# Decoder layer, second quantisation: block 0 rounded, turned and copied alone, block 1 behind the first MLP chunk

## What is computed

```python
x = _layernorm(x + attn(x, Wi, Wf, Wg, w_norm, Wo))          # "1" in the kernel's names
x = _layernorm(x + wkv(w, u, k=x, v=ctx))                    # "2"
x = _layernorm(x + ffn(x, w_gate_up, w_down))                # "3"

def ffn(x, w_gate_up, w_down):
    xq = quant(x)                       # per token: round(x / s) * s, s = max|x| / 127
    gate, up = split(xq @ quant(w_gate_up).T)                # 1408 each
    h = silu(gate) * up
    return quant(h) @ quant(w_down).T
```

## Time and profile before

| | before |
|---|---|
| time, median of 3 runs | 444.82 us (441.57 to 445.95) |
| the profiled execution: its time / its span | 447.09 us / 445.3 us |
| PE busy | 368.4 us (83%) |
| DVE busy | 367.7 us (83%) |
| ACT busy | 321.1 us (72%) |
| POOL busy | 233.1 us (52%) |
| chain that ended last, by engine | ACT 23%, PE 21%, DVE 20%, issue 18%, POOL 10%, DMA 5% |
| mean granted TensorE clock | 0.931 of 2.4 GHz |

### The profile page before, as it was taken

The page is one execution under the profiler, slowest core; times in us unless marked ns, Lnnn a source line. Parts: engine busy times, 40 slices in busy tenths (PEclk is TensorE's granted clock), DMA queues, the critical chain, the costliest instruction groups (busy, mean ns, idle before and its releaser), DMA issues.

```text
span 445.3 us, 7315 instructions
## 1 busy us (share of the span) xinstructions
PE 368.4 (83%) x2462; PEld 284.6 (64%) x2484; DVE 367.7 (83%) x620; ACT 321.1 (72%) x421; POOL 233.1 (52%) x283
## 2 busy tenths in 40 slices
PE   4895689299939989989998999899989998558773
PEld 4894579189736577748775877577757885224331
DVE  2869529966798889998989898979898989899684
ACT  4487286656954789859884988498859985886762
POOL 3436442463364475468446843673477437635550
PEclk8697888779997999999999999989999999978998
DMA  8659635136301002030203020302011101000101
GB/s 299 269 188 180 104 116 177 47 131 66 118 23 74 0 1 72 1 119 1 72 1 118 3 71 1 116 2 70 0 67 50 59 12 59 11 26 0 49 4 68
DMA packets 13340, 31.70 MB, mean 71 GB/s; under 512 B 4864, under 2 KB 4864, under 8 KB 13312
## 3 DMA queue, kind: packets, MB, share of 16 engines
q1 hardware_dynamic: 13312, 31.35, 23.3%
HBM read 27.14 MB, written 4.21 MB: 70 GB/s over the span
## 4 chain that ended last, share of the span: by engine, by line
ACT 23%; PE 21%; DVE 20%; issue 18%; POOL 10%; DMA 5%; POOLq 0%; ACTq 0%; DVEq 0%; SPq 0%
PE proj_ps L460 14%; PE slot_ps L561 4%; DMA ring<-w_gate_up_dram 3%; POOL ring L1207 3%; ACT L921 2%; ACT hqT L894 2%; ACT turn_ps L834 2%; ACT L925 2%; DVE inp L1396 2%; ACT ring L880 2%; DVE x_max L1512 2%; POOL x_low L1130 2%; ACT gate L775 2%; ACT turn_ps L842 1%; POOL gate L1147 1%
## 5 line engine op out<-in xcount | busy, mean ns | idle before, releaser
L561 PE MATMUL slot_ps<-w1q,xqT 128*128 128x512 bf16 (+1 forms) x377 | 84.4, 376 | 10.2 <-ACT xqT L871 7.6
L460 PE MATMUL proj_ps<-x_high,proj_high 128*128 128x256 f32 x384 | 67.3, 299 | 7.7 <-DVE inp L1415 3.8
L1207 POOL TENSOR_TENSOR ring<-ring 128x512 f32<-128x512 f32 (+1 forms) x48 | 60.4, 1261 | 21.4 <-ACT ring L880 21.4
L561 PEld LDWEIGHTS slot_ps<-w1q,xqT 128*128 128x128 bf16 x384 | 37.6, 101 | 50.1 <-issue 12.5
L460 PE MATMUL proj_ps<-x_low,proj_high 128*128 128x256 f32 x384 | 63.7, 289 | 0.0
L460 PE MATMUL proj_ps<-x_high,proj_low 128*128 128x256 f32 x384 | 63.6, 289 | 0.0
L460 PEld LDWEIGHTS proj_ps<-x_high,proj_high 128*128 128x128 f32 x384 | 55.8, 198 | 10.8 <-issue 9.4
L460 PEld LDWEIGHTS proj_ps<-x_high,proj_low 128*128 128x128 f32 x384 | 54.8, 196 | 0.0
L460 PEld LDWEIGHTS proj_ps<-x_low,proj_high 128*128 128x128 f32 x384 | 54.6, 195 | 0.0
L880 ACT ACTIVATE ring<-ring,zero_bias,x_scale 128x512 f32<-128x512 f32 (+1 forms) x48 | 37.0, 774 | 12.0 <-DVE ring L1535 11.8
L594 PE MATMUL slot_ps<-w2q,hqT 128*128 128x512 bf16 x161 | 38.5, 385 | 6.3 <-ACT hqT L894 4.3
(11 more groups left out here) (129 smaller groups left out, 825.3 us busy)
## 6 DMA issues: line engine op xcount, KB each, us to landing
ring<-w_gate_up_dram SPq DMA_DIRECT2D x11, 512.0 KB, 5.1
forget<-xT_dram SPq DMA_DIRECT2D x8, 512.0 KB, 3.7
x_sb<-x_dram SPq DMA_DIRECT2D x8, 512.0 KB, 4.0
c_sb<-cT_dram SPq DMA_DIRECT2D x8, 512.0 KB, 4.3
out_dram<-z SPq DMA_DIRECT2D x16, 256.0 KB, 2.1
ring<-w_down_dram SPq DMA_DIRECT2D x4, 704.0 KB, 5.2
scale_rows<-scratch_dram SPq DMA_DIRECT2D x2, 704.0 KB, 5.9
x<-wfT_dram SPq DMA_DIRECT2D x2, 512.0 KB, 5.0
```

The costliest lines, as they stand in the source:

```text
L460: last = nc.tensor.matmul(out, a, b, start=(i == 0), stop=(i == len(terms) - 1))
L561: last = nc.tensor.matmul(slot_ps[:, s, half * 512:half * 512 + width], xqT[:, par, d, t * P:(t + 1) * P], w1q[:, d, half * I + at:half * ...
L1207: nc.gpsimd.tensor_tensor(hid, hid, gate_buf[:, at:at + width], ALU.mult).then_inc(hid_ready, 1)
```

## The change

`turn_inputs` and `read_inputs` take a block as an argument, and every batch's second quantisation goes in two steps. In `iteration`, TensorE turns block 0 of the next batch between the two parts of block 0's down projection, and block 1 only in the next iteration, behind the first chunk of `mlp_up`. ScalarE rounds block 0, copies it, rounds block 1, does `normalise_1`, and then copies block 1. The two blocks lie in different banks of `turn_ps`. `mlp_up` waits for its own block, and `turn_keys` and `exponential` wait for both blocks. `xq_turned` and `xq_ready` now count blocks, not batches. Batches 0, 1, 6 and 7 are changed in the same sense in their written-out parts. No instruction of VectorE, GpSimd or SyncE is moved, added or removed.

```diff
-        turn_16 = turn_ps[:, 0:512].bitcast(F16).rearrange("p (c t) -> p c t", c=DB)
+        turn_16 = [turn_ps[:, 0:256].bitcast(F16), turn_ps[:, 768:1024].bitcast(F16)]
...
-                wait(pe, xq_ready, b)
+                wait(pe, xq_ready, 2 * b)
...
-            def turn_inputs(b):
-                pe.wait_ge(x2_rounded, 2 * b + 2)
+            def turn_inputs(b, t):
+                pe.wait_ge(x2_rounded, 2 * b + t + 1)
                 pe.wait_ge(z2_ready, 2 * b + 2)
                 for c in range(DB):
-                    for t in range(TB):
-                        last = nc.tensor.transpose(turn_16[:, c, t * P:(t + 1) * P],
-                                                   low_halves(z2[:, t, c * P:(c + 1) * P]),
-                                                   identity16[:, :])
+                    last = nc.tensor.transpose(turn_16[t][:, c * P:(c + 1) * P],
+                                               low_halves(z2[:, t, c * P:(c + 1) * P]),
+                                               identity16[:, :])
                 last.then_inc(xq_turned, 1)
...
-                        if t == 0:
-                            pe.wait_ge(xq_ready, b + 1)
+                        pe.wait_ge(xq_ready, 2 * b + t + 1)
...
-            def mlp_down(n, t):
+            def mlp_down(n, t, parts=(0, 1)):
...
                 mlp_up(b, par, 0, [0])
+                turn_inputs(b, 1)
                 mlp_up(b, par, 0, [1])
...
-                mlp_down(n, 0)
-                turn_inputs(b + 1)
+                mlp_down(n, 0, (0,))
+                turn_inputs(b + 1, 0)
+                mlp_down(n, 0, (1,))
...
-            turn_inputs(0)
+            turn_inputs(0, 0)
+            turn_inputs(0, 1)
...
-            turn_inputs(1)
-            mlp_down(0, 0)
+            mlp_down(0, 0, (0,))
+            turn_inputs(1, 0)
+            mlp_down(0, 0, (1,))
...
             mlp_up(6, 0, 0, [0])
+            turn_inputs(6, 1)
             turn_keys(7, 0)
...
             mlp_down(12, 0)
-            turn_inputs(7)
+            turn_inputs(7, 0)
             mlp_up(7, 1, 0, [0])
+            turn_inputs(7, 1)
             mlp_up(7, 1, 0, [1])
...
-            def read_inputs(b, par):
-                act.wait_ge(xq_turned, b + 1)
+            def read_inputs(b, par, t):
+                act.wait_ge(xq_turned, 2 * b + t + 1)
                 wait(act, mlp_done, (b - 1) * TB * NC)
-                nc.scalar.activation(xqT[:, par, :, :], turn_16, ACT.Identity,
-                                     bias=half_bias[:, :]).then_inc(xq_ready, 1)
+                nc.scalar.activation(xqT[:, par, :, t * P:(t + 1) * P],
+                                     turn_16[t].rearrange("p (c t) -> p c t", c=DB),
+                                     ACT.Identity, bias=half_bias[:, :]).then_inc(xq_ready, 1)
...
                 round_2(b + 1, 1 - par, 0)
+                read_inputs(b + 1, 1 - par, 0)
                 round_2(b + 1, 1 - par, 1)
-                read_inputs(b + 1, 1 - par)
                 normalise_1(b + 2)
+                read_inputs(b + 1, 1 - par, 1)
...
             silu(0, 0, 1, [1])
-            read_inputs(1, 1)
+            read_inputs(1, 1, 0)
             silu(0, 0, 1, [2])
             normalise_1(2)
+            read_inputs(1, 1, 1)
...
             round_2(7, 1, 0)
+            read_inputs(7, 1, 0)
             round_2(7, 1, 1)
-            read_inputs(7, 1)
+            read_inputs(7, 1, 1)
             normalise_3(11, 1)
```

More of the change, by code:

```diff
@@ L585, in turn_hidden @@
                 last.then_inc(hq_turned, 1)
-            def mlp_down(n, t):
+            def mlp_down(n, t, parts=(0, 1)):
                 s = (t + NC) % 2
-                pe.wait_ge(mlp_read, chunks_read(n))
-                for part, (first, count) in enumerate(PARTS):
+                if parts[0] == 0:
+                    pe.wait_ge(mlp_read, chunks_read(n))
+                for part in parts:
+                    first, count = PARTS[part]
                     pe.wait_ge(hq_ready, 2 * n + part + 1)
@@ L595, in mlp_down @@
                                                 start=(i == 0), stop=(i == IB - 1))
-                last.then_inc(down_done, 1)
+                if parts[-1] == 1:
+                    last.then_inc(down_done, 1)
             def turn_rows(q):
@@ L818, in exponential @@
                 act.wait_ge(k_turned, 2 * b + h + 1)
-                wait(act, xq_turned, b)
+                wait(act, xq_turned, 2 * b)
                 if isinstance(b, int) and b == 0:
@@ L1034, in _ @@
             read_projection(2, 1)
-            read_inputs(0, 0)
+            read_inputs(0, 0, 0)
+            read_inputs(0, 0, 1)
             normalise_1(1)
```

## The result

The changed kernel takes 447.11 us in the median of 20 runs (442.01 to 450.8), the kernel before, run beside it, 445.04 us (441.4 to 447.82). The ratio is 1.0069, 95% interval 1.0043 to 1.0095: slower by 3.1 us, within 1.9 and 4.2. It compares fast runs alone, and so is not the quotient of the two medians over all runs, which differ by 2.1 us (1.0047). The forecast was 2.0 us, slower but within 1%, and both held. Its size lies inside the interval, at its lower edge.

A forecast was written before the change was run, and what follows sets the result against it. The prediction took the path through `x_low` to `project`, not TensorE's bubble, as the bound. Its terms, 1.8 - 0.4 + 0.6 = +2.0 us on the 444.82 us median, gave 446.8 us, range 442.0 to 450.3 us.

The forecast's parts named there:

- The path over the border: Between iterations: VectorE statistics, GpSimd shift, ScalarE `normalise_1` and `split_x`, GpSimd `x_low`, TensorE `project`; TensorE's bubble beside it, 0.43 us spare.
- The half copy: ScalarE's copy of one block: 0.69 us; block 1's, between `normalise_1` and `split_x`, delays `x_high` by 0.59 to 0.69 us.
- Chunk 0 1.3 us earlier, TensorE's wait 1.2 us: At iteration 3's start: up projection's chunk 0 starts 1.3 us sooner, but TensorE then idles 1.2 us for `x_low`.
- Borders 2, 3 and 5 at +0.6, border 1 at 0: Starts of iterations 2, 3, 5: +0.6 us each from late `x_low`; iteration 1: 0, existing waits cover the copy.
- Border 4, -0.4: Start of iteration 4: TensorE at 1.2 GHz set the pace, so earlier chunk 0 brings `project` forward, -0.4 us.
- Batch 6, +0.6: Start of batch 6, no `split_x`: `turn_keys`, which waited for `normalise_1`, now also waits for the copy behind it, +0.6 us.
- third rival: Block 1 comes late: chunk 0 at 1.2 GHz delays `x_low`, or idling before `project` lowers the clock; 450.4 us, chance 0.12.
- Batch 7, 0: Block 0's copy 1.3 us earlier, rounding of hidden rows 0.7 us late; bounds -0.7 and +0.7 us, taken as 0.
- The loads ahead of the loop: Before the loop one copy becomes two, +0.2 us, swallowed by a wait for the context's DMA: 0.

The follow-up runs named there:

- The extra instruction: Changed kernel plus one unused 128x512 ScalarE copy between `normalise_1` and the copy of block 1, iterations 1 to 5: 1.0127 of the kernel before.
- the copy ahead of `normalise_1`: Changed kernel with block 1 turned right behind the down projection's second part and copied before `normalise_1`: 0.9965 of the kernel before (0.9927 to 1.0003).

## Why the prediction was right, point by point

The mechanism at the borders was right, and there the size too. The total came out near the forecast in part by luck: by the traces, the sum left out about 2 us behind border 6, and the difference of the two medians, 2.1 us, lies nearer to the forecast than the ratio's 3.1 us.

- **The path over the border: right.** Statistics, shift, `normalise_1`, `split_x`, `x_low`, `project`. The extra instruction shows that it is tight, and the copy ahead of `normalise_1` shows that nothing else of the change costs at the borders.
- **The half copy: right.** Predicted 0.69 us, median 0.686; its delay 0.59 to 0.69, measured 0.57, a little less, since the copy behind `normalise_1` took 0.66. The estimate from the Trainium skill (ScalarE: Activation LUTs, Rules for kernel authors), 0.72 us, is 5% above the row.
- **Chunk 0 1.3 us earlier, TensorE's wait 1.2 us: right** (1.3 and 1.20).
- **Borders 2, 3 and 5 at +0.6, border 1 at 0: right**, with +0.55 (45.50 against 44.95), and 45.27 against 45.29 us for the first period.
- **Border 4, -0.4: right in size** (45.50 against 45.96, -0.46), and less of an accident than I thought: each of four traces of before paid once for the low clock there or at border 2.
- **Batch 6, +0.6: the copy right, the term too small.** `turn_keys` came 0.66 us late. But the longer wait ahead of it stood in front of a stretch at 1.2 GHz in three traces of four. In the profiled one chunk 1 reached VectorE 4.51 us behind the start of `turn_keys` (379.22 to 383.73), before 2.85 us (381.34 to 384.19): 1.66 us more. The one trace without that stretch stands only 0.5 us above the trace of before with its low stretches in the most similar places (67.34 against 66.85 us from border 6 to the end); the three with it stand at 69.99 to 70.19 us. This is the term that was mis-sized: for batches 6 and 7 together the sum had +0.6 us, and the traces have +2.8 us in the mean. Whether the longer wait brings the low clock stays open, as said above. The prediction had named a low clock from TensorE's new idle time as part of its third rival, but looked for it ahead of `project`, where none of the four traces has it, and left it out at batch 6, where the new wait was twice as long.
- **Batch 7, 0: right in the profiled pair.** From the first rounding to the row maximum of the hidden rows (L1554 before, L1566 after) it took 12.34 us before (409.73 to 422.07) and 12.24 us after (409.60 to 421.84). VectorE read chunk 0 0.33 us earlier and the rounding of the hidden rows late by 0.47 us, and by the row maximum the two kernels were level again.

The sum over the traces: four periods of +0.55 are 2.2, less 1.05 for the low clock at a border, is the +1.15 us of the table's first column (the means are 227.31 and 226.16). Behind the shift of border 6 the means are 69.4 and 66.6, +2.8: 0.66 by the copy, 3/4 of 1.66 (1.2) by the low clock right behind it, and another 0.9 us further on. Every trace has three or four more low stretches there, at places that differ between the traces; I haven't worked out which of them the 0.9 us belong to. Together +4.0 us, beside the 3.1 (1.9 to 4.2) of the timed runs.

The loads ahead of the loop, which the sum put at 0, are neither borne out nor refuted: the shift of border 1 differs by up to 6.5 us between traces of one kernel.

The Trainium skill (Perfetto Trace Analysis, Optimizing Scalar/DVE Operations) says that breaking up the instructions of an unsaturated ScalarE that makes bubbles on other engines may let work complete sooner. Here chunk 0 came 1.3 us sooner and the kernel did not. It paid only when the engine with the bubble was last (440.99 to 438.54 us).

## What to carry to other kernels

Before an engine's bubble is removed, look at what that engine waits for next: here it waited 0.43 us for another path right behind the bubble, so an earlier start could gain nothing until that path was shorter. Splitting an instruction costs little, but every piece stands somewhere in an in-order queue; put the pieces into that engine's own waits, and never between two steps of the path. When a wait is lengthened on TensorE, price the matmuls behind it at 1.2 GHz as well, as a risk: here it came in four traces of seven.

## What the runs showed of the hardware

Between border 1 and border 6 the stretches at 1.2 GHz kept to few places: border 4 in three of four traces of the kernel before, border 2 in the other one, and border 6 in three of four of the changed one, with 5.31 us for 16 matmuls of 512 columns in place of 3.62, and 4.88 us for those of 512 and 384 in place of 3.19. Behind border 6 each of the eight traces has three or four more.

The part ahead of the loop differed more between executions of the same kernel than the change is worth: the shift of border 1 was at 149.88 to 153.37 us in four traces of the kernel before, and at 147.21 to 153.72 in four of the changed one, while from there to border 6 they agreed within 0.24 us. For a change inside the loop, the distance between two marks of the trace is the sharper measure.
